# Products of the softmax sums two steps later in a batched cross-attention kernel

## The reference

```
q = rms_norm(x @ q_w + q_b, nq_s)
k_txt = rms_norm(txt_ctx @ k_w + k_b, nkt_s);  v_txt = txt_ctx @ v_w + v_b
k_img = rms_norm(img_ctx @ ki_w + ki_b, nki_s); v_img = img_ctx @ vi_w + vi_b
out = (sdpa(q, k_txt, v_txt) + sdpa(q, k_img, v_img)) @ o_w + o_b
x = x + out;  x = x + ffn(layernorm(x))
```

## Time and profile before

| | us |
|---|---|
| median of 3 runs | 1920.23 (1919.83 to 1922.81) |
| profiled execution | 1918.63 |
| its span | 1916.8 |
| PE busy in the span | 1751.0 (91%) |
| DVE busy | 1397.1 (73%) |
| POOL busy | 1149.5 (60%) |
| ACT busy | 983.2 (51%) |

### The profile page before, as it was taken

How to read it: one execution, slowest core, us unless ns; L and a number is a source line. 1 busy time by engine, 2 the same in 40 slices (tenths; PEclk the granted TensorE clock), 3 DMA queues, 4 the chain that set the end, 5 groups by cost and what they waited for, 6 DMA issues and landing times. The chain is left out here.

```text
span 1916.8 us, 30691 instructions
## 1 busy us (share of the span) xinstructions
PE 1751.0 (91%) x8731; PEld 1534.5 (80%) x8731; DVE 1397.1 (73%) x2577; ACT 983.2 (51%) x1657; POOL 1149.5 (60%) x989
## 2 busy tenths in 40 slices
PE   7899979999999999999999999999992998699998
PEld 6566669889888888888898898888892886688887
DVE  4344477887978878878878879788782564577776
ACT  3444445555655655555555556556552553244443
POOL 1000278888788788788788887887862331133332
PEclk9999999999999999999999999999996999799999
DMA  3365564465564665554564665556436782133332
GB/s 110 121 208 197 194 183 111 107 116 123 123 120 114 130 121 117 122 135 114 116 132 108 116 126 125 116 116 131 98 90 195 252 274 92 66 107 115 116 109 78
DMA packets 417364, 251.19 MB, mean 131 GB/s; under 512 B 350272, under 2 KB 368832, under 8 KB 415520
## 3 DMA queue, kind: packets, MB, share of 16 engines
q1 hardware_dynamic: 417312, 250.55, 51.2%
HBM read 187.71 MB, written 60.10 MB: 129 GB/s over the span
## 5 line engine op out<-in xcount | busy, mean ns | idle before, releaser
L1322 ACT ACTIVATE p_high<-psum,key_rms 128x448 fp32r<-128x448 f32 x384 | 244.7, 637 | 397.1 <-PE psum L1145 397.0
L1143 PE MATMUL psum<-p_high,c_high 128*128 128x448 f32 (+1 forms) x768 | 287.8, 375 | 48.0 <-DVE p_low L1405 48.0
L1405 DVE TENSOR_TENSOR p_low<-psum,p_high 128x448 fp32r<-128x448 f32 x384 | 236.4, 616 | 100.2 <-ACT psum L1324 99.1
L1143 PE MATMUL psum<-u_high,c_high 128*128 128x448 f32 x768 | 285.5, 372 | 21.0 <-DVE psum L1416 15.1
L1144 PE MATMUL psum<-u_low,c_high 128*128 128x448 f32 x768 | 282.5, 368 | 0.0
L1145 PE MATMUL psum<-u_high,c_low 128*128 128x448 f32 x768 | 281.5, 366 | 0.0
L1145 PE MATMUL psum<-p_high,c_low 128*128 128x448 f32 (+1 forms) x768 | 281.5, 366 | 0.0
L1144 PE MATMUL psum<-p_low,c_high 128*128 128x448 f32 (+1 forms) x768 | 281.0, 366 | 0.0
L1416 DVE COPY psum<-beta_wide 128x448 f32<-128x448 f32 x416 | 259.4, 627 | 20.2 <-DMA beta_wide<-absorbed_biases 4.4
L1617 POOL TENSOR_TENSOR c_low<-stage,c_high 128x512 fp32r<-128x512 f32 x208 | 273.6, 1316 | 0.0
L1324 ACT ACTIVATE psum<-psum,key_rms 128x448 f32<-128x448 f32 x384 | 232.3, 605 | 0.0
(11 more groups left out here) (241 smaller groups left out, 4018.3 us busy)
## 6 DMA issues: line engine op xcount, KB each, us to landing
stage<-in_ctx SPq DMA_DIRECT2D x210, 256.0 KB, 2.8
averages<-o_raw SPq DMA_DIRECT2D x64, 448.0 KB, 5.2
o_stage<-averages SPq DMA_DIRECT2D x32, 896.0 KB, 5.4
u_raw<-absorbed_queries SPq DMA_DIRECT2D x60, 448.0 KB, 5.5
absorbed_queries<-u_stage SPq DMA_DIRECT2D x14, 1792.0 KB, 6.8
beta_wide<-absorbed_biases SPq DMA_DIRECT2D x32, 448.0 KB, 5.3
recip_wide<-reciprocals SPq DMA_DIRECT2D x32, 448.0 KB, 4.1
p_wide<-probs_by_expert SPq DMA_DIRECT2D x32, 448.0 KB, 3.6
```

The lines of the kernel that those rows point to most:

```text
L1143: nc.tensor.matmul(out, high, rhigh, start=start, stop=False, **kw)
L1322: nc.scalar.activation(p_high[:, probs_slot(u), :], src, ACT.Exp, scale=key_rms[:, t:t + 1])
L1405: return nc.vector.tensor_tensor(out, a, b, ALU.subtract)
```

## The change

The lists of steps move. Product and copy of each sum come two steps later, so do the reciprocals and the scaling of the image half of o_raw. The splitting of the sums stays at its steps.

```diff
-        TEXT_SUM_SPLIT, TEXT_SUMS, TEXT_RECIP = (1, 2), (3, 5), 10
-        IMAGE_SUM_SPLIT, IMAGE_SUMS, IMAGE_RECIP = (7, 8), (9, 11), 16
+        TEXT_SUM_SPLIT, TEXT_SUMS, TEXT_RECIP = (1, 2), (5, 7), 12
+        IMAGE_SUM_SPLIT, IMAGE_SUMS, IMAGE_RECIP = (7, 8), (11, 13), 18
...
-                    if step in (20, 22):
-                        scale_o(it, IMAGE, (step - 20) // 2)
+                    if step in (22, 24):
+                        scale_o(it, IMAGE, (step - 22) // 2)
```

## The result

The changed kernel takes 1961.47 us (median of 4 runs, 1960.12 to 1962.06), against 1921.3 for the kernel before in the same comparison (1919.83 to 1922.81): a ratio of 1.0208, interval 1.019 to 1.0226. That is 40 us slower, where 1959 was predicted. The profiled execution took 1960.12, 41.5 more than that of before (1918.63).

The account below looks back on a forecast made before the run. PE sets the pace, but in each batch's first half it waits for DVE, itself held by POOL. 14 middle batches by 2.69 make 37.7, first and last 1.3 together: 39.0 on 1918.6, so 1959 as median; range 1937 to 1970.

Parts of the forecast that it names:

- The late scaling makes DVE 1.08 later: Steps 24 to 1: POOL scales o_raw first, about 2.1 us, so the CAST and subtraction of step 1 end 1.08 later.
- The CAST and subtraction of step 2 get short, and 0.84 is won: Steps 2 to 4: both run at short lengths, and PE takes p_low of unit 2 at 859.61, not 860.45.
- The chain from norm to norm is 5.46: POOL's key_root, big product, c_low and c_twice between DVE's norms: 5.4 to 5.5 us at step 4, 5.46 at step 10.
- PE waits 2.2 at step 5, 1.35 at step 11, about 1 at step 14: PE waits for the norm before the sums, then for p_low; batch 1.4 later at step 5, 2.69 by step 14.
- The terms of the lone row are blocked: Step 12: behind take(11), DVE's two terms meet POOL's u_low and c_low; L1479 and L1482 take over 1 us each.
- the first rival: Rival (a): DVE's CAST now starts ahead of POOL's u_low, so the kernel gets faster, 1879 us; chance 0.07.
- the clock: PE's clock was to stay at 1.00 (2.4 GHz) in the middle; a fall was rival (d), chance 0.03.
- Rival (a): Faster: CAST ahead of u_low, waits of 1.46 and 1.26 go, 41 us off, 1879; chance 0.07.
- Rival (b): No change: wins at steps 4 and 10 pay for the sums' waits, terms don't collide; 1920 within 4; chance 0.04.
- Rival (c): Only the scaling at step 24 costs, DVE's order is absorbed: 5 to 16 us, about 1930; chance 0.07.
- Rival (d): PE's clock falls once a batch, losing 1.8 us each time, 27 on top of the 39: 1986; chance 0.03.
- the waits named in the prediction's second paragraph: PE's waits in the kernel before: 1.46 at step 4, 0.92 at step 8, 1.26 at step 10, each ended by DVE.

## Why the prediction was right, step by step

**The late scaling makes DVE 1.08 later.** The norm of step 2 was put at 857.64 in the time of before, and stands at 857.48. The CAST of step 1 took 0.90, where its start and end gave 1.05. Alone the scaling costs 25 us. In the changed kernel the prediction's instants of steps 2 to 14 all carry this 1.08, and the trace bears them: without the late scaling the sum of step 5 comes 1.2 earlier. Yet taking it out gives nothing back, since a wait of 1.27 to 1.45 comes in its place at step 0. Going by its own terms the prediction would have put that kernel some 15 us below the changed one, and it is 5 above. It lets DVE catch up before the next batch. With the norm in its new place that holds only because the change also takes the big product out of step 20, which the prediction didn't weigh: there its sum came out right by luck.

**The CAST and subtraction of step 2 get short, and 0.84 is won.** 0.39 and 0.63, and PE takes the average of step 4 at 879.77, which is 859.46 in the time of before: 0.99 won.

**The chain from norm to norm is 5.46.** 883.22 less 877.79 is 5.43 at step 4, 901.32 less 895.85 is 5.47 at step 10, and 906.58 less 901.32 is 5.26 at step 12 (predicted 5.25). This was the core of the argument, and the runs bear it: the order of the norm alone costs 43 us (of its 2.8 a batch about half is the wait at step 0 that the changed kernel doesn't have), and taking the big product out of the chain in the changed kernel gives 21 back, with the waits ahead of the sums of steps 5 and 11 gone.

**PE waits 2.2 at step 5, 1.35 at step 11, about 1 at step 14.** Measured 2.05, 1.22 and 0.64. By step 5 the batch is 1.22 late (883.71 - 20.31 - 862.18), 1.4 predicted. At step 14 it is 2.36 late (912.21 - 20.31 - 889.54), 2.69 predicted, and 2.5 in the whole period (76.95 against 74.45). Of the 0.33 too much, half is there from step 2 on (its norm stands 0.16 earlier than forecast, that of step 8 0.19, that of step 12 0.17), and the rest lies in the terms of the lone row: the second took 1.49, not about 1.7.

**The terms of the lone row are blocked.** 1.23 and 1.49, over 1 each as forecast. The run that puts them back gives 13 us, 0.9 in each of 14 batches. The Trainium skill (SBUF — State Buffer, Who interferes with whom) says that whichever engine starts first holds the shared interface for its whole instruction. The trace agrees: the same L1482 takes 0.69 ahead of a POOL product and 1.49 and 2.41 behind one. But the rule that made the first rival is about one pair of instructions. Here the 0.99 that the shorter CAST won at step 4 was lost again at step 5, because the norm's chain and not DVE's work was last.

**Where the forecast was wrong in part: the clock.** I wrote that it stays at 1.00, with the fall as a rival of 0.03. It falls in ten batches of 16, each time within 1.7 us of the end of the wait of 2.0 at step 5. Two windows of the changed kernel from the end of that wait on, one in a batch with and one in a batch without:

```profile
574.29:578.19 3.90, 3.90 (x11) 3.33 (x12) 3.77 (x7) 1.16 (x2) 3.85 (x3) 0.58 0.26 67
883.71:887.61 3.90, 3.90 (x20) 3.32 (x21) 3.77 (x7) 1.57 (x3) 3.87 (x3) 1.00 0.24 67
```

In the first, PE is at the level of 1.2 GHz for most of the stretch and issues 11 matmuls in place of 20. The twelfth starts 4.02 behind the first, in the other batch 2.54: 1.5 us lost. Of these only about 0.5 are left at the end of the batch, since PE has waits ahead of it anyway: the sum of step 7, which waited 0.35 in the other batch, starts here at 580.74 with no idle time. So the 41.5 are made up: 14 periods longer by 2.53 (35.4; 76.98 in the mean of the short ones against 74.45), the first longer by 1.8 (77.1 against 75.27), and nine of the 15 longer by another 0.47 for the clock (4.2). The prediction's sum had 39.0 by 2.69 a batch and no clock; the one error covered half of the other, and that 1959 lies only 2.5 off is luck to that extent. The Trainium skill (TensorE: Matmul & The Clock Gate, A second HAM failure mode: psum-queue depth-cycling) tells of a kernel whose clock swings under frequent short idling. Here the fall comes with one wait of 2 us, and the kernel with more but shorter waits (the norm's place alone, none over 1.6 behind the first batch) has no fall in the middle.

**What costs how much.** The edits don't add up. Over their own kernel before, the scaling alone is 25 us, the lists alone 10, both 31; the place of the norm alone 43, with the lists 45, and with both 40. Whatever stood beside it, the norm's place brought the time to 40 to 45 above before (the scaling beside it without the lists wasn't run). That isn't because the other edits cost nothing then: with the norm's new place the late scaling costs 1.2 us ahead of step 5 and saves about as much at step 0. The clock is in all these figures: some 3 us in the scaling alone, 5 in the lists alone, none in the norm's place alone, 4 in the change.

**The rivals.** Rival (a) would have needed the norm of step 4 at about 860.8; it stands at 862.91 (883.22 - 20.31). Rival (b) needed the waits ahead of L1214 to be short; they are 47.5 us between 300 and 1380. Rival (c) held the order of DVE for absorbed; alone it costs 43. Rival (d) came in part, at 4 us in place of 27. What I had not weighed is that the waits named in the prediction's second paragraph can be had back without touching the sums: POOL's big products a step later, no longer ahead of DVE's CAST and subtraction, are worth 40 us on the kernel before.

## What to carry to other kernels

On an engine that works in order, look at what stands between a value that others wait for and the instruction that makes the next one; a big product without a near taker belongs behind it, not ahead of it. When a table of steps moves, ask which order is computed from it: here the moved sums cost 10 us by themselves, and 45 with the norm's place that was worked out from their lists. If taking an edit back gives nothing, compare the instants in the two traces before calling it free: the late scaling cost 1.2 us in one half of the batch and saved them in the other. And a shorter instruction, or an engine with less busy time, says nothing as long as another chain ends last.

## What the runs showed of the hardware

Within `attend` (from 255 us on) the granted clock fell to the level of 1.2 GHz only about the end of a wait of PE of 1.87 us or more, from 0.7 ahead of that end to 1.7 behind it, and not with every such wait. The matmuls then start 0.37 apart in place of 0.21. Behind the first batch:

| kernel | waits, us | falls |
|---|---|---|
| changed | 15 of 2.04 to 2.21 | 10 |
| only the late scaling | 15 of 2.00 to 2.05 | 7 |
| lists and nothing else | 14 of 1.87 to 2.01, one of 1.77 | 9 |
| lists and the norm's place, no late scaling | 15 of 1.88 to 2.21 | 5 |
| changed, old place of the norm | 15 of 1.99 to 2.05 | 5 |
| changed, terms by the norm | 15 of 2.04 to 2.21 | 5 |
| changed, u_low later | 15 of 2.68 to 2.77 | 15 |
| only the norm's place | none over 1.6 | 0 |

The last idles more in all than the changed kernel (85 us of waits against 69, from 300 to 1380 us). In the first batch single waits of 2.69 (before) and 3.54 (changed) went without a fall, and one of 2.30 (before with two products late) had one. What picks the waits that have one the records don't tell.

An instruction of DVE from SBUF to SBUF that has to wait for POOL's lengthens by whatever is left of it: L1479 took 0.45 and 1.23, the CAST 0.38, 0.50, 0.90 and 1.34, the same instruction each time. Three of these long ones end 0.24 to 0.25 behind POOL's big product: the CAST of step 2 before (858.24 and 857.99), and in the changed kernel the CAST of step 1 (874.52 and 874.28) and L1479 (909.99 and 909.74). A mean over such a group mixes the two kinds.
